# Linear attention in steps of two head pairs on array quarters, and one clock fill fewer in each LSTM step

## The reference, cut to what matters

```
i, f, g, o = split(x[:, t] @ Wx + h @ Wh + b)
c = sigmoid(f) * c + sigmoid(i) * tanh(g)
h = sigmoid(o) * tanh(c)
```

```
q, k, v = heads(x @ wq.T), heads(x @ wk.T), heads(x @ wv.T)
phi(z)  = exp(z @ omega.T - 0.5 * sum(z * z)) / 8
out     = sum_{j<=i} (phi(q_i) . phi(k_j)) v_j  /  (sum_{j<=i} phi(q_i) . phi(k_j) + 1e-6)
x       = x + concat(out) @ wo.T + bo
```

## Time and profile before

| | us |
|---|---|
| median of 3 runs | 6295.27 |
| profiled execution, its own time | 6286.49 |
| its span, first to last instruction | 6284.7 |
| lstm1, lstm2, lstm3 | 882 to 1226, 2009 to 2354, 2903 to 3248 |
| linear attention | 1227.4 to 1995.1 |
| mean granted TensorE clock | 0.960 of full speed |

### The profile page before, as it was taken

The page is one execution under the profiler, slowest core; times in us unless marked ns, Lnnn a source line. Parts: engine busy times, 40 slices in busy tenths (PEclk is TensorE's granted clock), DMA queues, the critical chain, the costliest instruction groups (busy, mean ns, idle before and its releaser), DMA issues. The chain is left out here.

```text
span 6284.7 us, 114370 instructions
## 1 busy us (share of the span) xinstructions
PE 5601.0 (89%) x38798; PEld 4322.7 (69%) x38989; DVE 2978.1 (47%) x8233; ACT 2475.4 (39%) x6283; POOL 133.2 (2%) x340
## 2 busy tenths in 40 slices
PE   7997699999999997889989988888888868888999
PEld 5773347788887775556757865687777848855666
DVE  3552322355554225663247743566666667543111
ACT  4442222233333225773224433355555535433333
POOL 1000000000000000000000000000000010000000
PEclk9999889999999998999989999899999989998999
DMA  0000000000000000000000000000000000000000
GB/s 33 0 0 18 0 18 0 0 1 0 0 0 7 0 0 0 0 0 24 0 0 1 0 3 0 1 1 2 2 1 2 1 39 0 0 0 0 0 0 13
DMA packets 2984, 26.62 MB, mean 4 GB/s; under 512 B 321, under 2 KB 833, under 8 KB 1473
## 3 DMA queue, kind: packets, MB, share of 16 engines
q1 hardware_dynamic: 2768, 23.76, 1.0%
HBM read 21.66 MB, written 2.10 MB: 4 GB/s over the span
## 5 line engine op out<-in xcount | busy, mean ns | idle before, releaser
L573 PE MATMUL banks<-clock_fill 128*128 128x512 bf16 x2509 | 695.5, 387 | 11.5 <-issue 1.1
L342 PE MATMUL banks<-attn_value,attn_probs_turned 128*128 128x144 f32 x3072 | 448.3, 289 | 0.7 <-ACT attn_probs_turned L402 0.2
L573 PEld LDWEIGHTS banks<-clock_fill 128*128 128x128 bf16 x2700 | 295.1, 113 | 214.3 <-issue 13.5
L623 PEld LDWEIGHTS banks<-act_a,weights 128*128 128x128 f32 x3048 | 399.2, 191 | 61.7 <-DVE act_a L669 7.6
L342 PE MATMUL banks<-cells_value,cells_probs_turned 128*128 128x136 f32 x3072 | 419.6, 280 | 0.2 <-ACT cells_probs_turned L402 0.2
L402 ACT ACTIVATE attn_probs_turned<-banks 128x512 f32<-128x512 f32 x384 | 229.6, 599 | 453.2 <-PE banks L331 453.1
L342 PEld LDWEIGHTS banks<-cells_value,cells_probs_turned 128*128 128x128 f32 x3072 | 397.8, 190 | 10.6 <-ACT cells_probs_turned L402 0.5
L342 PEld LDWEIGHTS banks<-attn_value,attn_probs_turned 128*128 128x128 f32 x3072 | 397.4, 190 | 5.7 <-ACT attn_probs_turned L402 2.0
L402 ACT ACTIVATE cells_probs_turned<-banks 128x512 f32<-128x512 f32 x384 | 229.6, 598 | 384.6 <-PE banks L331 384.6
L623 PE MATMUL banks<-act_a,weights 128*128 (+1 forms) x3048 | 375.0, 274 | 3.2 <-DVE act_a L669 3.2
L662 DVE TENSOR_TENSOR lstm_fc<-lstm_c,lstm_sig 128x32 f32<-128x32 f32 x384 | 73.8, 192 | 620.3 <-ACT lstm_sig L645 620.3
(11 more groups left out here) (403 smaller groups left out, 10644.2 us busy)
## 6 DMA issues: line engine op xcount, KB each, us to landing
weights<-in_p SPq DMA_DIRECT2D x1, 2894.5 KB, 16.1
weights<-in_p SPq DMA_DIRECT2D x1, 2894.0 KB, 9.6
weights<-in_p SPq DMA_DIRECT2D x2, 1364.0 KB, 8.5
x_res<-in_x SPq DMA_DIRECT2D x1, 2048.0 KB, 12.7
out_x<-x_res SPq DMA_DIRECT2D x1, 2048.0 KB, 6.3
weights<-in_p SPq DMA_DIRECT2D x1, 1836.0 KB, 11.0
weights<-in_p SPq DMA_DIRECT2D x1, 1835.5 KB, 7.0
weights<-in_p SPq DMA_DIRECT2D x1, 1344.5 KB, 9.7
```

The source lines that it names most:

```text
L342: last = pe.matmul(ps[:, CTX, bb * span:(bb + 1) * span], et[:, g, t * P:(t + 1) * P], vt[:, p, bb, h * span:(h + 1) * span], start=(g == ...
L573: pe.matmul(core.ps[:, FILL, :], core.fill[:, 0:P], core.fill[:, :], start=True, stop=True)
L623: last = pe.matmul(ps[:, first + parity, lo:lo + NB].unsqueeze(1), w("Wh", g * P, P), state, start=False, stop=True, skip_group_check=True)
```

## The change

Each LSTM step issues three clock fills in place of four (L630). `FIRST_FILLS`, the leaky unit and the GRU keep theirs.

Linear attention takes two pairs of heads (four heads) in a step: 4 steps per batch, 128 in all, five deep.

- q and k of both pairs go into one PSUM bank of 512 columns (before: two banks in turn, 256 columns each). DVE copies and ACT squares 512 columns at a time.
- `features` uses only the 64 x 64 blocks that are not zero, each on its own quarter of the array. For pair a and half hh the rows are 64*hh onwards; the output columns are the same half for a = 0 and the opposite half for a = 1. So the four products lie on the four quarters; pair a writes bank PHI + a. The pass over `omegaT` goes over all four quarters, then that over `half_block`.
- `scores` does four 64-row products of 128 columns into two banks; the halves of pair 1 are swapped, which `sums` undoes with `3 - h`.
- `value` is one matmul of 256 columns; `sums` is four matmuls of 65 columns without padding, each with its own start and stop; `turn` is two transposes; DVE and ACT handle double widths.
- On PE, the waits of `features` (q and k copied and squared, exp of the step before done) stand ahead of `project`; then come `project`, `turn`, `features`, `scores`, `value`, `sums`, `output`. `turn` of step n-4 follows `sums` of step n-4, which ended the previous round, and stands behind `project`; `output` comes last. ACT's order is turned copy, square, exp; DVE's is q/k copy, mask, v, normalise, output.

The core of the diff (the double widths on DVE and ACT, the orders just named, and the tile shapes are left out):

```diff
@@ lstm_stage, PE
-                fill_clock(pe, core, 4)
+                fill_clock(pe, core, 3)
@@ linear_attention_stage
-    PHI, VAL, SCORE, SUMS, OUT = 2, 3, 4, 6, 7
-    DEPTH = 6
-    SPAN = 2 * (DH + 1)
-    steps = NB * NJ
+    NP = NJ // 2
+    QK, VAL, PHI, SCORE, SUMS, OUT = 0, 1, 2, 4, 6, 7
+    DEPTH = 5
+    HEADS = 4
+    steps = NB * NP
...
+        def quarters():
+            for a in range(2):
+                for hh in range(2):
+                    rows = slice(DH * hh, DH * (hh + 1))
+                    cols = rows if a == 0 else slice(DH * (1 - hh), DH * (2 - hh))
+                    yield a, rows, cols
...
             def project(st):
                 if st.m == 0:
                     pe.wait_ge(s["source_ready"], st.u + 1)
-                x, bank = src[:, slot(st), :], st.m % 2
-                past(pe, s["sq_ready"], st.n - 1)
-                pe.matmul(ps[:, bank, 0:P], w("wqT", st.m * P, P), x, start=True, stop=True)
-                pe.matmul(ps[:, bank, P:2 * P], w("wkT", st.m * P, P), x, start=True, stop=True).then_inc(
-                    s["qk_done"], 1)
+                x = src[:, slot(st), :]
+                past(pe, s["sq_ready"], st.n)
+                for a in range(2):
+                    for t, name in enumerate(("wqT", "wkT")):
+                        last = pe.matmul(ps[:, QK, (2 * a + t) * P:(2 * a + t + 1) * P],
+                                         w(name, (2 * st.m + a) * P, P), x, start=True, stop=True)
+                last.then_inc(s["qk_done"], 1)
...
+                pe.matmul(ps[:, VAL, 0:2 * P], src[:, slot(st), :], w("wvT", 2 * st.m * P, 2 * P), start=True,
+                          stop=True).then_inc(s["v_done"], 1)
+
+            def features_wait(st):
+                pe.wait_ge(s["qk_ready"], st.n + 1)
+                pe.wait_ge(s["sq_ready"], st.n + 1)
+                past(pe, s["phi_ready"], st.n)
 
             def features(st):
                 p = st.m % 2
-                pe.wait_ge(s["qk_ready"], st.n + 1)
-                past(pe, s["phi_ready"], st.n)
-                pe.matmul(ps[:, PHI, 0:2 * P], w("omegaT"), qk[:, p, :], start=True, stop=False)
-                pe.wait_ge(s["sq_ready"], st.n + 1)
-                pe.matmul(ps[:, PHI, 0:2 * P], const("half_block"), sq[:, p, :], start=False, stop=True).then_inc(
-                    s["phi_done"], 1)
+                for a, rows, cols in quarters():
+                    pe.matmul(ps[cols, PHI + a, 0:2 * P], w("omegaT", rows.start, DH, rows=DH, first=rows.start),
+                              qk[rows, p, 2 * a * P:2 * (a + 1) * P], start=True, stop=False)
+                for a, rows, cols in quarters():
+                    last = pe.matmul(ps[cols, PHI + a, 0:2 * P],
+                                     const("half_block", rows.start, DH, rows=DH, first=rows.start),
+                                     sq[rows, p, 2 * a * P:2 * (a + 1) * P], start=False, stop=True)
+                last.then_inc(s["phi_done"], 1)
 
             def scores(st):
...
+                for a in range(2):
+                    for half in range(2):
+                        rows = slice(DH * half, DH * (half + 1))
+                        last = pe.matmul(ps[:, SCORE + half, a * P:(a + 1) * P], phi[rows, p, a, 1, :],
+                                         phi[rows, p, a, 0, :], start=True, stop=True)
                 last.then_inc(s["s_done"], 1)
 
             def sums(st):
...
-                for hh in range(2):
-                    last = pe.matmul(ps[:, SUMS, 0:SPAN], sm[:, st.m % 2, hh, :], vt[:, st.m % 4, hh, :],
-                                     start=(hh == 0), stop=(hh == 1))
+                for h in range(HEADS):
+                    a, half = h // 2, h % 2 if h < 2 else 3 - h
+                    last = pe.matmul(ps[:, SUMS, h * (DH + 1):(h + 1) * (DH + 1)], sm[:, st.m % 2, half, a, :],
+                                     vt[:, st.m % 4, h, :], start=True, stop=True)
...
             def body(p):
-                for st, part in ((p[0], project), (p[1], features), (p[0], value), (p[2], scores)):
-                    if st is not None:
-                        part(st)
-                if p[5] is not None and p[5].m == NJ - 1:
-                    output(p[5])
-                for st, part in ((p[3], sums), (p[4], turn)):
-                    if st is not None:
-                        part(st)
+                if p[1] is not None:
+                    features_wait(p[1])
+                if p[0] is not None:
+                    project(p[0])
+                if p[4] is not None:
+                    turn(p[4])
+                if p[1] is not None:
+                    features(p[1])
...
+                if p[4] is not None and p[4].m == NP - 1:
+                    output(p[4])
```

More of the change, by code:

```diff
@@ L1828, in linear_attention_stage @@
         src = sb("src", [P, 2, P])
[L1829 to L1838, removed]
+        qk = sb("qk", [P, 2, BANK])
+        sq = sb("square", [P, 2, BANK])
+        phi = sb("features", [P, 2, 2, 2, P])
+        vt = sb("value", [P, 4, HEADS, DH + 1])
+        sm = sb("masked", [P, 2, 2, 2, P])
+        den = sb("denominator", [P, HEADS])
+        inv = sb("inverse", [P, HEADS])
+        o = sb("context", [P, 2, 2, P])
         ot = sb("context_turned", [P, NJ, P])
@@ L1924, in turn @@
                     past(pe, s["out_read"], st.u)
-                pe.transpose(ps[:, OUT, 0:P], o[:, st.m % 2, :], const("ident")).then_inc(s["ct_done"], 1)
+                for a in range(2):
+                    last = pe.transpose(ps[:, OUT, a * P:(a + 1) * P], o[:, st.m % 2, a, :], const("ident"))
+                last.then_inc(s["ct_done"], 1)
             def output(st):
@@ L1929, in output @@
                 for j in range(NJ):
-                    last = pe.matmul(ps[:, OUT, P:2 * P], w("woT", j * P, P), ot[:, j, :], start=(j == 0),
+                    last = pe.matmul(ps[:, OUT, 2 * P:3 * P], w("woT", j * P, P), ot[:, j, :], start=(j == 0),
                                      stop=(j == NJ - 1))
@@ L1950, in square @@
                 past(act, s["phi_done"], st.n - 1)
-                act.activation(sq[:, st.m % 2, :], ps[:, st.m % 2, 0:2 * P], ACT.Square).then_inc(s["sq_ready"], 1)
+                act.activation(sq[:, st.m % 2, :], ps[:, QK, :], ACT.Square).then_inc(s["sq_ready"], 1)
             def features(st):
@@ L1963, in turned @@
                     past(act, s["out_done"], st.u)
-                act.activation(ot[:, st.m, :], ps[:, OUT, 0:P], ACT.Copy).then_inc(s["ct_ready"], 1)
+                act.activation(ot[:, 2 * st.m:2 * st.m + 2, :], ps[:, OUT, 0:2 * P].rearrange("p (a j) -> p a j", a=2),
+                               ACT.Copy).then_inc(s["ct_ready"], 1)
             def body(p):
-                for st, part in ((p[0], square), (p[1], features), (p[4], turned)):
-                    if st is not None:
-                        part(st)
+                if p[4] is not None:
+                    turned(p[4])
+                if p[0] is not None:
+                    square(p[0])
+                if p[1] is not None:
+                    features(p[1])
             run(act, body)
@@ L1975, in _ @@
             wait_pack(dve, core, 2)
-            dve.memset(vt[:, :, :, :], 0.0).then_inc(s["ones_ready"], 1)
+            dve.memset(vt[:, :, :, DH:DH + 1], 1.0).then_inc(s["ones_ready"], 1)
             dve.wait_ge(s["ones_ready"], 1)
[L1978 to L1981, removed]
             def query_key(st):
@@ L2018, in output @@
                 xb = core.x[:, tok(st.u * P, P)]
-                dve.scalar_tensor_tensor(out=xb, in0=ps[:, OUT, P:2 * P], scalar=w("bo"), in1=xb, op0=ALU.add,
+                dve.scalar_tensor_tensor(out=xb, in0=ps[:, OUT, 2 * P:3 * P], scalar=w("bo"), in1=xb, op0=ALU.add,
                                          op1=ALU.add).then_inc(s["out_read"], 1)
             def body(p):
[L2023 to L2027, removed]
+                if p[0] is not None:
+                    query_key(p[0])
+                if p[2] is not None:
+                    mask(p[2])
+                if p[0] is not None:
+                    value(p[0])
                 if p[3] is not None:
                     normalise(p[3])
+                if p[4] is not None and p[4].m == NP - 1:
+                    output(p[4])
             run(dve, body)
```

45 lines of the change are left out of this document (23 added, 22 removed).

## The result

| | before | changed |
|---|---|---|
| median, us | 6293.9 (4 runs, same chip) | 6733.1 (6731.9 to 6736.7, 4 runs) |
| profiled span | 6284.7 | 6730.2 |
| first to last state (`h`) of lstm1, lstm2, lstm3 | 343.1, 343.1, 343.3 | 532.7, 534.4, 532.7 |
| linear attention | 767.7 | 642.9 |

The changed kernel is slower: ratio 1.070 (95% interval 1.068 to 1.072), where 0.967 was forecast. The three LSTMs lost 189.6 + 191.3 + 189.4 = 570 us, linear attention gained 125 us; together 445, which is the whole difference of the spans (445.5). Short spells of low clock in stages that nothing touched come and go between executions of most kernels here and move their times by up to 50 us, so that differences of stages are read from the stages' own spans.

What follows compares the result with a forecast made beforehand. PE was taken to bound both changed stages, with fills setting the LSTM step's start. LSTMs -78 us and linear attention -126 us took 6286.5 to 6082, placed at 6088 us; range 6040 to 6200.

Steps and rivals of the forecast that it cites:

- Cost: nothing: LSTM steps: dropping one fill costs nothing; if the clock did halve, each recurrent pass would double; no chance given.
- LSTM arithmetic: LSTM step: one fill of 0.215 us removed from a pitch of 2.71, PE's round then 2.495 us.
- The gap from state to load: LSTM step: 0.12 us from finished state to next recurrent weight load, taken from the leaky unit; 0.26 before.
- the recurrence's own bound: LSTM step without PE's fills: 2.24 + 0.12 + 0.11, together 2.47 us, just under PE's round.
- The 78 us: Forecast gain of the three LSTM stages together: 26.7 us per stage, 0.7 given back at loop turns.
- Linear attention: Linear attention stage: rounds of 4.57 us, including a 0.2 wait before the transposes; 642 us against 767.7, a gain of 126.
- Quarters: Linear attention features: four quarter-array products run at once despite the bank rule, 0.86 us plus 0.2 for change of shape.
- Two at a time: Rival, linear attention features: quarters run only in twos, by bank conflict or shared rows; + 110 us, 6198; chance 0.18.
- one at a time: Rival, linear attention features: quarters serialise fully; + 330 us, 6418; chance 0.05.
- a longer wait: Rival, linear attention: the context before the transposes comes later; 0.5 us more per round, + 64, 6152; chance 0.10.
- The LSTMs' lack of gain: Rival, LSTM steps: state to load stays 0.26 us, so nothing is gained; + 78 us, 6166; chance 0.05.
- The slower outcome that I listed: The only rival slower than the kernel before: feature quarters serialise fully in linear attention, 6418 us; chance 0.05.

Runs made afterwards that it cites:

- e5: Changed kernel with four fills per LSTM step and the bias matmul left out, so results are not the model's; 6096 us.
- e8: Changed kernel, three fills kept, with the LSTM bias matmul on all 128 rows in place of 4; 6064 us.
- e7: Changed kernel with four fills per LSTM step and the bias matmul on all 128 rows in place of 4; 6088 us, ratio 0.965.
- e2: Changed kernel with four fills per LSTM step again, so the new linear attention alone; 6175 us, ratio 0.981.
- f1: Changed kernel with four fills, and features by 128 x 128 block-diagonal matrices in place of quarters; 6254 us, ratio 0.993.
- e6: Changed kernel with three fills per LSTM step, but eleven in every eighth step; 6669 us.
- e4: Changed kernel with four fills of 448 columns per LSTM step in place of three of 512; 6805 us, ratio 1.079.
- e11: Changed kernel, three fills kept, with the LSTM bias matmul left out, so results are not the model's; 6427 us.

## Why the prediction was wrong

- *The clock, "Cost: nothing".* This is the step that failed, and it alone put the forecast wrong. I reasoned from PE's busy share (341.2 of 345.9 us, and the leaky unit's 179.1 of 248.0 at 0.98) that the fills' clock was safe. Both readings were of the wrong quantity. The changed LSTM has PE busy for all of 524.6 us and loses the clock; e5 with PE idle at times keeps it. The leaky unit was no proof of safety: its 0.98 is the mean of full clock and three short spells at half clock. And it has four fills in each 1.9 us (248 us for its 128 steps); an LSTM step has them in 2.71, beside recurrent passes that are bound by weight loads at 32 columns each and a bias matmul on four rows. I named the price ("each recurrent pass would double") and gave it no chance and no place among the rivals. Recurrent passes did go from 0.11 to 0.21 us, the pitch from 2.50 to 4.27, and the three LSTMs lost 570 us.
- *LSTM arithmetic.* Right while the clock lasted: pitch 2.50 in the first steps. The gap from state to load (0.12, measured 0.13 in e8) and the recurrence's own bound (2.47, measured 2.48) came out too, for the loop; in the written-out steps they are 0.05 and 2.31. The 78 us were there to be had (e7's LSTMs are together 82 us shorter than e2's), only not by taking a fill away with nothing in its place.
- *Linear attention.* Right in mechanism and in sum: 642.9 us against 642, round 4.51 against 4.57, features 1.03 against 1.06. That it came within 1 us is in part luck. The transposes cost 0.15 more than forecast, value and sums together 0.15 less; rounds were shorter by 0.06 us or more, while the stage ran at low clock for its first 9 us, left behind by lstm1, and its last 9. The first 9 cost little: e2 has 3 us of low clock there and takes 642.4.
- *Quarters.* Four at a time in the trace, and f1 prices them at 91 us by the stage's span. The Trainium skill's rule on PSUM banks (TensorEngine Tiling (Array Packing), Restrictions and Gotchas) did not bite: its words would forbid two row tiles in bank 2 at once, yet they start together here, where each half of the output partitions has one row tile per bank. Two row tiles in one bank and the same partitions were not tried.
- *Rivals.* Two at a time, one at a time and a longer wait did not occur. The LSTMs' lack of gain did not come from the gap between state and load. The slower outcome that I listed was the wrong one.

## What to carry to other kernels

An instruction whose output nobody reads may hold the clock; before it goes, ask what else in the same microseconds fills the array over all its rows, and list the loss of the clock as a rival with its full price. Look for work around it that can be made to count first: here the bias matmul on 128 rows with zeros cost 0.3 us less per step and kept the clock with one fill fewer. A mean clock just below full can hide short spells at half clock; look for them before reading it as safe. Start-to-start distances from a timeline priced a restructured stage to within 1%, changes of tile shape (0.15 to 0.2 us each) included, with single terms off by up to 0.15 us. Compare the stage's own span where the time of the whole moves by more than the effect.

## What the runs showed of the hardware that I had not expected

- Being busy did not keep PE's clock. The Trainium skill (TensorE: Matmul & The Clock Gate, Part 1) has the clock depend on how busy PE has recently been, and its advice (Why this matters for your kernels) is to avoid idle gaps. Here PE was busy for 524.6 of 524.6 us at 0.50, and e5 and e8 had gaps at 1.00. Busy is meant as the profile counts it, with the way through the array in a matmul's length; the clock itself may go by another measure.
- The loss lasts. At 1.2 GHz the same step takes 4.27 us in place of 2.50 and streams still less per microsecond, which may be why; nothing in the stage brings the clock back, only the burst of eleven fills in e6, for a few steps.
- The edge is close: 64 of 512 columns less in each fill (e4) lost the clock, after some 40 us in lstm1 and after two steps in lstm2 and lstm3, and cost 8% of the whole program.
- A matmul with 128 rows, 124 of them zeros, costs less time than one with 4 rows between neighbours on all rows (0.3 us less per step in e7, changes of shape included). With it three fills hold the clock, without it they do not (e8 and e11).
